# Decays of the last two sequences repeated by ScalarE, the last values moved to another PSUM bank, and a new written-out order of work

## What is computed

```python
# block 0, for each sequence
x = x + attention(ln(x) @ w_qkv, self mask) @ w_ao           # a, turn 0: 16 heads of 16
x = x + attention(ln(x) @ w_q, enc @ w_kv, cross mask) @ w_co  # a, turn 1
x = x + gelu(ln(x) @ w1 + b1) @ w2                            # b, turn 0
# block 1: a recurrence over the tokens, 32 heads of 8, from a given state s
xn = ln(x); sx = shift(xn) - xn; xxx = tanh((xn + sx*maa_x) @ maa_w1)
x5 = xn + sx * (maa_stack + xxx @ maa_w2)                     # five mixed streams
w = exp(-exp(time_decay + tanh(x5[1] @ dec1) @ dec2))         # the decays
r, k, v, g = x5[3] @ Wr, x5[0] @ Wk, x5[2] @ Wv, silu(x5[4] @ Wg)
out_t = r_t . (u * k_t v_t + s);  s = k_t v_t + w_t * s       # token by token
x = x + (groupnorm(out) * gn_w + gn_b) * g @ Wo
xn = ln(x); ... x = x + sigmoid(xr @ Wr2) * (relu(xk @ Wk2)**2 @ Wv2)
```

## Time and profile before

| what | value |
|---|---|
| median of 3 runs | 681.06 us (681.04 to 683.58) |
| the profiled execution | 682.92 us |
| its span | 681.1 us |
| granted TensorE clock, mean | 0.989 |
| instructions | 17297 |
| PE, PEld, DVE, ACT, POOL busy | 94%, 82%, 88%, 84%, 46% of the span |

### The profile page before, as it was taken

The page is one execution under the profiler, slowest core; times in us unless marked ns, Lnnn a source line. Parts: engine busy times, 40 slices in busy tenths (PEclk is TensorE's granted clock), DMA queues, the critical chain, the costliest instruction groups (busy, mean ns, idle before and its releaser), DMA issues.

```text
span 681.1 us, 17297 instructions
## 1 busy us (share of the span) xinstructions
PE 641.1 (94%) x5877; PEld 559.5 (82%) x5877; DVE 599.8 (88%) x1430; ACT 569.1 (84%) x2069; POOL 310.2 (46%) x440
## 2 busy tenths in 40 slices
PE   6889999999999999999999999999999989798876
PEld 5667788898888888988888888889889878688665
DVE  3699589999999999999999999999999997977674
ACT  1678999899999999999999999999999988664612
POOL 1254362546464554636364645446363644432220
PEclk9999999999999999999999999999999989999979
DMA  9920040310404050503122130505040222502200
GB/s 345 296 73 10 2 120 21 111 32 17 125 24 118 1 141 1 140 10 97 45 87 63 39 103 3 140 1 141 1 131 12 79 62 63 148 1 63 78 9 8
DMA packets 55293, 50.44 MB, mean 74 GB/s; under 512 B 6062, under 2 KB 50982, under 8 KB 54822
## 3 DMA queue, kind: packets, MB, share of 16 engines
q1 hardware_dynamic: 55206, 49.34, 24.8%
HBM read 28.62 MB, written 3.93 MB: 48 GB/s over the span
## 4 chain that ended last, share of the span: by engine, by line
PE 69%; ACT 16%; DVE 8%; issue 4%; DMA 1%; POOL 1%; SPq 0%; DVEq 0%; ACTq 0%
PE PS_B L730 14%; PE PS_T L832 8%; PE PS_S L730 6%; ACT SC L1473 5%; PE PS_B L872 5%; PE PS_D L737 5%; PE PS_T L840 4%; PE PS_S L803 4%; PE PS_S L737 3%; PE PS_T L737 3%; ACT PT L1483 2%; PE PS_D L978 2%; PE PS_D L730 2%; PE PS_T L723 2%; PE PS_B L894 2%
## 5 line engine op out<-in xcount | busy, mean ns | idle before, releaser
L1473 ACT ACTIVATE SC<-SC,NMX 128x128 f32<-128x128 f32 x512 | 200.1, 400 | 1.6 <-DVE NMX L1157 1.4
L1473 ACT ACTIVATION_READ_ACCUMULATOR SC<-SC,NMX 128x1 f32 x512 | 102.0, 199 | 0.0
L832 PE MATMUL PS_T<-CST,SC 128*128 128x128 f32 x512 | 81.0, 281 | 10.5 <-ACT SC L1473 6.2
L1157 DVE TENSOR_REDUCE NMX<-SC 128x4 f32<-128x512 f32 x128 | 84.1, 668 | 2.9 <-POOL SC L1680 1.9
L1483 ACT ACTIVATE PT<-PS_T 128x512 f32<-128x512 f32 x120 | 71.3, 594 | 11.5 <-PE PS_T L832 9.7
L832 PEld LDWEIGHTS PS_T<-CST,SC 128*128 128x128 f32 x512 | 56.6, 142 | 28.4 <-ACT PT L1483 14.7
L1238 DVE TENSOR_TENSOR_SCAN SS<-W,AJ 128x1024 f32<-128x1024 f32 x32 | 73.1, 2286 | 2.4 <-DMA W<-EW 1.7
L730 PE MATMUL PS_B<-MX,W 128*128 128x128 f32 x512 | 64.8, 276 | 1.1 <-ACT KR L1532 1.0
L1680 POOL TENSOR_TENSOR SC<-SC,MADD 128x512 f32<-128x512 f32 x48 | 60.1, 1278 | 6.9 <-DVE SC L1137 6.7
L730 PEld LDWEIGHTS PS_B<-MX,W 128*128 128x128 f32 x512 | 60.7, 192 | 1.8 <-ACT KR L1532 1.2
L730 PE MATMUL PS_B<-B_LT,W 128*128 128x128 f32 x512 | 61.2, 278 | 0.5 <-ACT B_LT L1411 0.4
(11 more groups left out here) (229 smaller groups left out, 1622.0 us busy)
## 6 DMA issues: line engine op xcount, KB each, us to landing
W<-EW SPq DMA_DIRECT2D x32, 512.0 KB, 4.1
V<-values_by_head SPq DMA_DIRECT2D x28, 512.0 KB, 5.7
W<-in_weights SPq DMA_DIRECT2D x1, 4160.0 KB, 18.1
ENC<-in_enc SPq DMA_DIRECT2D x16, 128.0 KB, 3.7
out<-X SPq DMA_DIRECT2D x16, 128.0 KB, 4.4
values_by_head<-VC SPq DMA_DIRECT2D x14, 128.0 KB, 2.1
X<-in_x SPq DMA_DIRECT2D x1, 1664.0 KB, 22.4
W<-in_weights SPq DMA_DIRECT2D x1, 1280.0 KB, 8.6
```

The source lines that it names most:

```text
L832: last = pe.transpose(PS_T[:, j * T:(j + 1) * T], SC[:, nr(b, a) % 2, g, j, :], ident)
L1157: dve.tensor_reduce(NMX[:, nr(b, a) % 2, GH * g:GH * g + GH], SC[:, nr(b, a) % 2, g], AX_X, ALU.max, negate=True)\
L1473: last = act.activation(SC[:, nr(b, a) % 2, g, j, :], SC[:, nr(b, a) % 2, g, j, :], ACT.Exp, bias=NMX[:, nr(b, a) % 2, h:h + 1], accum_out ...
```

## The change

Five edits.

```diff
 KEEP_WARM = {
...
-    ('d_out', 0, 14): 2, ('d_turn', 0, 14): 0, ('d_keyrec', 0, 14): 0, ('d_val', 0, 14): 2,
-    ('d_own', 0, 15): 2, ('d_read', 0, 15): 2,
+    ('d_turn', 0, 14): 0, ('d_keyrec', 0, 14): 0, ('d_own', 0, 15): 2, ('d_read', 0, 15): 0,
...
             def b_wspread(b, _):
+                if b < B - LAST:
...
             def b_valgate(b, k):
                 if k:
+                    if b == B - 1:
+                        pe.wait_ge(b_kr, B)
                     to_channels(PS_B[:, 0, C:2 * C], "g", C, 0, MX[:, 4]).then_inc(b_vgps, 1)
-                else:
+                elif b < B - 1:
                     pe.wait_ge(b_kr, b + 1)
                     pe.wait_ge(b_mx, 3 * b + 3)
                     to_channels(PS_B[:, 0, 0:C], "v", C, 0, MX[:, 2])
+                else:
+                    pe.wait_ge(a_res, 2 * B)
+                    pe.wait_ge(b_mx, 3 * B)
+                    to_channels(PS_T[:, 0:C], "v", C, 0, MX[:, 2]).then_inc(b_vgps, 1)
...
             def d_scan(b, t):
                 if t == 0:
                     dve.wait_ge(d_s0, b + 1)
-                    dve.wait_ge(b_w8, 32 * b + 32)
+                    dve.wait_ge(b_w8, 32 * b + (32 if b < B - LAST else 16))
+                elif b >= B - LAST:
+                    dve.wait_ge(b_w8, 32 * b + 32)
...
             def b_decays(b, _):
                 act.wait_ge(b_wd, b + 1)
                 act.wait_ge(b_w8, 32 * b)
-                act.activation(EW[:, :, 1:T], DW[:, :, 0:T - 1], ACT.Exp, scale=-1.0).then_inc(b_ew, 1)
+                if b < B - LAST:
+                    act.activation(EW[:, :, 1:T], DW[:, :, 0:T - 1], ACT.Exp, scale=-1.0).then_inc(b_ew, 1)
+                else:
+                    act.wait_ge(d_s, 2 * b)
+                    for t in range(CT):
+                        step = DW[:, t, 0:T - 1].unsqueeze(1).to_broadcast([P, RS, T - 1])
+                        act.activation(W8[:, t, :, 1:T], step, ACT.Exp, scale=-1.0).then_inc(b_w8, 16)
                 if b == B - 1:
                     act.activation(EARLY[:, 4:5], EW[:, 0, 0:1], ACT.Sqrt)
...
+                made = PS_B[:, 0, 0:C] if b < B - 1 else PS_T[:, 0:C]
+                act.activation(VC[:, :, :], tiles(made), ACT.Copy).then_inc(b_v, 1)
...
             def b_gatetanh(b, _):
-                act.wait_ge(b_vgps, b + 1)
+                act.wait_ge(b_vgps, b + 1 if b < B - 1 else B + 1)
```

More of the change, by code:

```diff
@@ L108 @@
[L108 to L112, removed]
@@ L232 @@
+    ("b_decays", 0, 45582), ("b_keyrec", 0, 45743), ("d_first_states", 0, 46553), ("b_values", 0, 46636),
+    ("b_gatetanh", 0, 46936), ("d_own", 0, 52493), ("d_ocopy", 0, 53464), ("d_squares", 0, 55206),
+    ("d_root_of", 0, 56778), ("d_affine", 0, 57497), ("d_scale", 0, 59521), ("d_root", 0, 59911),
+    ("d_keyrec", 0, 61327), ("d_relu2", 0, 61618),
 ]
 ACT_MOVED = {
-    ("a_scale", 0): {0: -50000, 1: -59980, 2: 9699, 4: 8467}, ("a_key", (0, 0)): {3: 10368, 15: 10481},
-    ("a_val", 0): {0: -49998, 1: -59972, 2: 10283, 4: 10625, 5: 11222, 15: 11155},
@@ new lines @@
+    ("b_decays", 0): {0: 43809, 1: 44876, 2: 47218, 4: 46278, 5: 44530, 6: 45885, 7: 45235, 8: 45818, 11: 44334,
+        12: 45342, 13: 43592, 14: 45789, 15: 48407},
+    ("b_keyrec", 0): {0: 43967, 1: 44865, 4: 45983, 5: 45235, 8: 45936, 11: 43872, 12: 45490, 13: 43771, 14: 42625},
+    ("d_first_states", 0): {1: 44311, 2: 42451, 5: 48146, 6: 45420, 10: 44082},
+    ("b_values", 0): {0: 46633, 1: 45763, 2: 46434, 3: 47655, 4: 47301, 7: 46376, 8: 46499, 9: 45881, 11: 45318,
+        12: 45566, 13: 44346, 14: 43559},
@@ new lines @@
+    ("a_root", 1): {1: 19320, 2: 22522, 4: 17861, 5: 20456, 8: 19101, 9: 23856, 10: 22685, 12: 22530, 13: 22872,
+        15: 19773},
+    ("a_addbias", 1): {0: 28891, 5: 20461, 8: 24970, 9: 23909, 12: 22658, 15: 32947},
+    ("a_addmask", (1, 0)): {0: 26180, 1: 22427, 4: 23913}, ("a_addmask", (1, 1)): {0: 26881, 1: 22431, 4: 24162},
+    ("a_addmask", (1, 2)): {0: 28282, 1: 22433, 2: 25719},
+    ("b_root", 0): {0: 30218, 3: 31570, 7: 34988, 11: 33144, 15: 32949},
+    ("b_addbias", 0): {0: 32429, 3: 33242, 15: 32951},
@@ L687, in b_wspread @@
             def b_wspread(b, _):
[L688 to L691, removed]
+                if b < B - LAST:
+                    sp.wait_ge(b_ew, b + 1)
+                    sp.wait_ge(d_s, 2 * b)
+                    for t in range(CT):
+                        sp.dma_start(W8[:, t], EW[:, t, :].unsqueeze(1).to_broadcast([P, RS, T])).then_inc(b_w8, 16)
             def a_load(b, _):
```

416 lines of the change are left out of this document (225 added, 191 removed), and 7 rows, old and new, of the table PE_MOVED.

## The result

The changed kernel takes 679.46 us (median of 8 runs, 677.57 to 680.22) against 681.95 us of the kernel before in the same runs (8 runs): a ratio of 0.9960, interval 0.9946 to 0.9974. It is 2.5 us faster where 4.9 were forecast. That is within the range given, but half the size, and under the 0.5% named as the bound.

A forecast was written before the change was run, and what follows sets the result against it. TensorE's work was taken to bound the middle, leaving the other stretches to win: 0.5 + 1.3 + 3.15 = 4.95, say 4.9 us, from the median of 681.06 to 676.2 us. Range 673 to 681.5.

The forecast's parts named there:

- The step that failed: Between 120 and 520 us: TensorE's work bounds it, a new order can at best keep it full; nothing won.
- The rival that the middle opens: 120 to 520 us: late pieces find little cover, 0.8 us a sequence over twelve sequences, giving 685.8 us; chance 0.08.
- the three signs of being wrong: Middle idle over 5 us; an Exp over 2 us; read.15 waiting for something other than its scan or keyrec1.14.
- The start: At 80.12 us: turn1.0 moved ahead of val.3 closes low1.0's 0.54 us wait for XX; 0.5 us won, between 0 and 2.
- Near 592 us: TensorE's 3.08 us wait for sequence 15's probabilities: low1.14 starts at 597.8 instead of 599.13, 1.3 us won, bounds 0 and 2.
- From low1.14 on: Everything since 600 us: OH of 15 starts at 660.35 instead of 663.50, 3.15 us won; the chain behind it unchanged.
- The scans' terms: From scan.15 at 648.5 us, scans, products and steps between, less overlaps, end at 658.3, 1.0 us earlier than before.
- The wide Exp at 1.0 us: Near 615 us: each 128x1016 Exp on ScalarE taken as 1.0 us, 3.2 at most, which would lose 4 us.
- mlp1.15 as what is late next: Near 615 us: the Exps stand ahead of the scale feeding mlp1.15, which comes 0.3 us later.
- The transfers: Removing the decays' transfer of 14, near 615 us, loses 0.1 us; that of 15 was hidden, its removal gives nothing.
- the third rival: Every table load holds ScalarE twice: OH comes 1.28 us later, the squares 0.7, giving 678.2 us; chance 0.05.
- The clock: If it falls behind the new 1.85 us gap after b_turn1.15, some 2.5 us of products cost double: 678.7; chance 0.17.

The follow-up runs named there:

- experiment 3: Changed kernel with only the transfer queue's (SP's) order put back to the old one: 680.48 us, ratio 0.9979 to the kernel before.
- experiment 5: Changed kernel with only VectorE's pieces between about 115 and 490 us in the old order: 686.57 us, ratio 1.0079 to the kernel before.
- experiment 6: Changed kernel with only ScalarE's pieces between about 115 and 490 us in the old order: 687.84 us, ratio 1.0096 to the kernel before.
- experiment 7: Changed kernel with only TensorE's pieces between about 115 and 490 us in the old order: 683.43 us, ratio 1.0029 to the kernel before.
- experiment 1: Changed kernel with the old turn numbers on all five queues, so the edits without the new order: 685.86 us, ratio 1.0054 to the kernel before.
- experiment 11: experiment 2 with sequence 14's decays repeated by the transfer again: 677.88 us, ratio 0.9952 to the kernel before.
- experiment 2: Changed kernel with all queues' pieces from about 115 to 527 us in the old order: 676.81 us, ratio 0.9923 to the kernel before.
- experiment 4: Kernel before with the new turn numbers and warmings, without the code edits: 682.76 us against 682.42, ratio 1.0021.
- experiment 8: experiment 2 without the two lines that load Sqrt behind the decays of 15: 677.84 us, ratio 0.9941 to the kernel before.
- experiment 10: Changed kernel with all queues in the old order from about 305 to 490 us alone: 678.90 us, ratio 0.9964 to the kernel before.

## Why the forecast was half right

**The step that failed** is the first: "The middle is bound by TensorE's work ... nothing is to be won in the middle: a new order there can at best keep TensorE full", and then no term for it in the sum. It was right that nothing could be won. But "at best" was then counted as the case, at zero. The runs show 1.81 us lost between mlp1.2 and mlp1.13, in every kernel with the new middle (411.39 to 411.47) and in none with the old (409.60 to 410.11), and the old middle put back gives 409.97 and a time of 676.81. The argument took TensorE's busy 397.9 of 400 us for proof that the order had nothing to do with the middle's length; 1.09 of the 1.81 us lie in busy time. The sign that was to show it, over 5 us of idle time, was therefore set on the wrong quantity: idle time is 2.6 of the 400 us, and none of the three signs of being wrong came. The rival that the middle opens had the right mechanism and named the place; its price, 0.8 us a sequence, was five times the 0.16 measured. At the measured price the forecast would have been 676.2 + 1.8 = 678.0, 3.1 us won against the 2.5 measured. What in the new order costs the 1.81 us stays open; experiments 3 and 5 to 7 exclude the stores and, each alone, the orders of VectorE, ScalarE and TensorE; POOL's was not tried alone.

**The start**: 0.5 forecast. That the table has 0.50 up to mlp1.0 is luck: the gap to be closed lies at 80.12 us, behind mlp1.0, and up to mlp1.0 the two kernels with the old start take 66.24 and 65.57 us, the twelve with the new one 65.19 to 66.83. The gap did close: low1.0 starts without a wait, and from mlp1.0 to mlp1.1 the twelve take 33.59 to 33.61 us, the two 34.14. The mechanism was right, with 0.54 us. But from mlp1.1 to mlp1.2 the changed kernel gives 0.48 of it back (37.33 against 36.85), which the forecast had not looked at.

**Near 592 us**: 1.3 forecast, 1.21 measured from mlp1.14 to low1.14 (15.17 to 13.96). The way differs in detail: XK came at 594.73, 1.1 us later than worked out, since VectorE had waited 0.45 us for the values' transfer and ran a scan first; TensorE's 3.08 us gap became 2.73 before keyrec.12 and 1.03 before low1.14, but at full clock (1.16 for keyrec.12's products, 1.91 before). In ten of the eleven experiments with this order the distance is 13.42 us, 1.75 less than before; the profiled execution of the changed kernel has the wait of 0.45 us on top.

**From low1.14 on**: 3.15 forecast up to OH.15, 2.95 measured (64.37 to 61.42). The scans' terms, from 648.5, add up to 658.4 and not to 658.3 less an overlap; the product's end came at 658.45, since scan.15 began 0.4 later than worked out and its product took 1.22 instead of 1.45. Behind OH.15 0.3 us were lost (17.6 to 17.9), with none forecast: half clock reaches the turn of OH.15 and the product behind it (0.68 and 1.36 us, before 0.44 and 1.03), and the experiments where these run at full clock have 17.6 to 17.7 too, but for experiment 1. The wide Exp at 1.0 us was right, so was mlp1.15 as what is late next: its wait for B_LT was 0.3 in the forecast and cost 0.6 (18.29 to 18.90 us from low1.14); in experiment 11, without the Exps, mlp1.15 follows mlp1.14 1.0 us sooner than in experiment 2.

**The transfers**: that of 14 was priced at 0.1 lost; by the rows of experiment 11 about 0.5 is lost (1.0 paid for 0.5), not separated from nothing by the medians. That of 15 was called hidden, true of the old order; experiment 4 shows 2.07 us of wait for it in the new one. The 3.15 us stood on it without a term of its own.

**The added loads**: the third rival, that each holds ScalarE twice, is refuted: the Exp of the changed kernel follows its load of 1.28 us at 590.16 by 0.01 us (591.45), and experiment 8 takes the load out of the end without moving what waits there. The Trainium skill's drain (ScalarE: Activation LUTs, What ACT_TABLE_LOAD costs) is not seen in any of these rows.

**The clock**: keyrec.14 waits 4.05 us (5.0 worked out). Half clock follows for its products and for read.15, as the forecast had counted (658.3 to 660.2), and for the two rows behind OH.15. Behind the new gap of 1.84 us, which the rival was about, the clock stayed full in the changed kernel, and the mean clock is 0.992, before 0.989. In experiments 4, 7 and 11 it fell there; in 7 and 11 that cost 1.3 us up to the first select, about half of the rival's 2.5.

**The sum as measured**: 0.50 + 1.21 + 2.95 won, 1.66 lost between mlp1.0 and mlp1.14 (1.81 less 0.06 and 0.09) and 0.3 behind OH.15, is 2.7, the difference of the two spans. Without the 0.50 of luck it is 2.2; the medians, 2.5, hold the chance of several executions.

## What to carry to other kernels

When an edit comes with a new order of everything, compare the distances between landmarks of the work, period by period: a fixed window with the same busy share hid 1.8 us here. Price a reordering of a full engine as a loss with a size, not as zero, and try the new order only where it is needed: the new ends with the old middle gave 0.8% where the change gave 0.4%. An edit and an order can each lose alone (0.5% and 0.2% slower) and pay together, so undo them one at a time before judging either. And read a forecast's term at its own place: a sum can be met by a number from somewhere else.

## What was not expected of the hardware

TensorE's granted clock falls at some places in some executions and not in others with the same gaps ahead. Behind two gaps of 1.55 and 0.69 us near 557 us, the 32 products of PT and VP took 1.92 to 1.94 us in the kernel before and experiments 8 and 10, 1.25 and 1.26 in the changed one and experiment 4, and 1.08 in the other nine; TensorE in the kernel before:

```profile
556.32 0.63 PE L832 MATMUL PS_T<-CST,SC 128*128 128x128 f32 x4 [1.55 <-ACT SC L1473]
557.64 1.94 PE L840 MATMUL PS_T<-PT,VP 128*32 128x128 f32 x32 [0.69 <-ACT PT L1483]
```

and in experiment 2:

```profile
555.25 0.63 PE L1121 MATMUL PS_T<-CST,SC 128*128 128x128 f32 x4 [1.54 <-ACT SC L1770]
556.57 1.08 PE L1129 MATMUL PS_T<-PT,VP 128*32 128x128 f32 x32 [0.69 <-ACT PT L1780]
```

Sequence 13's period is then 36.9 to 37.1 or 35.4 to 35.6 us. The other places: behind the gap of 1.84 us ahead of the product of KK, full clock in nine profiled kernels and half in three (experiments 4, 7 and 11); read.15 at 1.94 or 1.07 us; keyrec.15 in experiment 1. These 1 to 2 us of chance at each place lie on top of every comparison here: experiment 2's profiled run has the better case near 557 us and the changed kernel's the worse, so that 1.6 of the 4.5 us between their spans lies in that period. The ratios of the medians are the numbers to trust for the whole; the middle's 1.4 us between the two (411.41, 409.97) lies ahead of that place, where the clock is full in both. Six of the changed kernel's eight executions have a mean clock of 0.992 and two of 0.997, experiment 2's six all 0.995: whether the order has a part in where the clock falls, and whether one can be made that keeps it, was not tried.
